# Ending a mixture-of-experts kernel with accumulating DMAs into the output, and splitting the last four scatters over two sums

## The reference, cut to what matters

```
x = x + attention(ctx_512, layernorm(x))
xn = layernorm(x)
routed = zeros(T, 512)
for e in experts:                       # 64
    routed[token_of[e]] += (silu(g) * u) @ down[e] * weight[e]    # g, u = xn[token_of[e]] @ gate_up[e]
shared = silu(xn @ shared_gate.T) * (xn @ shared_up.T) @ shared_down.T
x = x + routed + shared                 # 2048 x 512 float32, 4 MiB
```

## Time and profile before

| | us |
|---|---|
| median of 3 runs | 582.22 (580.47 to 582.86) |
| the profiled execution's own time | 581.39 |
| its span in the trace | 579.8 |
| busy: PE, DVE, ACT, POOL | 536.4, 245.3, 161.8, 224.6 |
| last scatter issued | 547.84 |
| first load of the even sum issued | 552.79 |
| last addition on DVE ends | 573.55 |

### The profile page before, as it was taken

How to read it: one execution, slowest core, us unless ns; L and a number is a source line. 1 busy time by engine, 2 the same in 40 slices (tenths; PEclk the granted TensorE clock), 3 DMA queues, 4 the chain that set the end, 5 groups by cost and what they waited for, 6 DMA issues and landing times.

```text
span 579.8 us, 6266 instructions
## 1 busy us (share of the span) xinstructions
PE 536.4 (93%) x2087; PEld 290.6 (50%) x2087; DVE 245.3 (42%) x641; ACT 161.8 (28%) x342; POOL 224.6 (39%) x221
## 2 busy tenths in 40 slices
PE   4999999678799999999999999999999999999835
PEld 2545545444355555555555555555555555554312
DVE  0786779999612232222222321223222322325535
ACT  3775797673011111211111111111211111120000
POOL 3052155642343354434444444434633363432200
PEclk9999999999999999999999999999999999999969
DMA  8947386789277999989999999999999999868487
GB/s 278 355 167 274 85 290 222 278 300 364 65 271 210 312 280 303 285 261 327 286 278 308 329 299 274 331 277 269 316 300 273 303 308 326 224 121 261 90 298 298
DMA packets 53704, 155.06 MB, mean 267 GB/s; under 512 B 7264, under 2 KB 8800, under 8 KB 52128
## 3 DMA queue, kind: packets, MB, share of 16 engines
q1 hardware_dynamic: 34944, 109.74, 52.3%
q0 software_dynamic: 16320, 40.39, 30.1%
q10 hardware_dynamic: 2400, 4.46, 2.2%
HBM read 116.28 MB, written 38.28 MB: 267 GB/s over the span
## 4 chain that ended last, share of the span: by engine, by line
PE 57%; DMA 18%; DVE 10%; issue 8%; SPq 2%; ACT 2%; POOL 2%; POOLq 0%; DVEq 0%; ACTq 0%
PE bank L870 22%; DMA out<-y,table 12%; PE bank L727 7%; PE bank L738 6%; PE bank L855 4%; PE bank L829 4%; PE bank L640 4%; PE bank L852 3%; PE bank L845 3%; DMA raw_down<-in_sh_down 3%; DMA odd_sum<-y,table 3%; DVE bn L1130 1%; DVE x L1127 1%; PE bank L836 1%; DVE ones_hi L1192 1%
## 5 line engine op out<-in xcount | busy, mean ns | idle before, releaser
L870 PE MATMUL bank<-gu_w,gxT 128*128 128x384 f32 x512 | 178.9, 493 | 2.2 <-ACT gxT L1058 2.2
L870 PEld LDWEIGHTS bank<-gu_w,gxT 128*128 128x128 f32 x512 | 93.2, 190 | 79.8 <-issue 28.9
L563 POOL DMA_INDIRECT out<-y,table x34 | 54.1, 1591 | 199.6 <-DVE y L1360 166.2
L1346 DVE TENSOR_TENSOR hid<-bank,eg 128x192 f32<-128x192 f32 x64 | 22.9, 358 | 178.9 <-ACT eg L1066 178.9
L1066 ACT ACTIVATE eg<-bank 128x192 f32<-128x192 f32 x64 | 21.2, 332 | 275.6 <-PE bank L870 275.6
L727 PE MATMUL bank<-xnT,upT 128*128 128x512 f32 x192 | 86.2, 595 | 1.6 <-ACT sg L973 1.5
L569 POOL DMA_INDIRECT gx<-rows_dram,table x64 | 63.1, 985 | 27.7 <-issue 19.2
L1360 DVE TENSOR_SCALAR y<-bank,gx 128x512 f32<-128x512 f32 x64 | 45.1, 746 | 54.1 <-PE bank L855 54.1
L640 PE MATMUL bank<-w,h1T 128*128 128x512 f32 x128 | 57.7, 593 | 0.0
L738 PE MATMUL bank<-downT,shid 128*128 128x512 f32 x96 | 44.9, 611 | 11.6 <-DVE shid L1232 11.6
L727 PEld LDWEIGHTS bank<-xnT,upT 128*128 128x128 f32 x192 | 34.9, 190 | 39.1 <-issue 36.4
(11 more groups left out here) (179 smaller groups left out, 511.5 us busy)
## 6 DMA issues: line engine op xcount, KB each, us to landing
gu_w<-in_gate_up SPq DMA_DIRECT2D x64, 768.0 KB, 6.8
dn_w<-in_down SPq DMA_DIRECT2D x32, 768.0 KB, 5.4
x<-in_x SPq DMA_DIRECT2D x4, 1024.0 KB, 14.0
feat_dram<-feat SPq DMA_DIRECT2D x16, 256.0 KB, 3.4
out<-shid SPq DMA_DIRECT2D x8, 512.0 KB, 4.1
odd_sum<-shid SPq DMA_DIRECT2D x8, 512.0 KB, 4.9
rows_dram<-rows ACTq DMA_DIRECT2D x4, 1024.0 KB, 10.0
gu_w<-out SPq DMA_DIRECT2D x4, 1024.0 KB, 8.1
```

The costliest lines, as they stand in the source:

```text
L563: pool.indirect_dma_start(sums[lane(e)], bass.IndirectOffsetOnAxis(ap=table[:, e:e + 1], axis=0), y[:, e % YB, :], None, compute_op=ALU.ad ...
L870: last = nc.tensor.matmul(GU[e % 2][:, 0:2 * I], gxT[:, e % 2, c, :], gu_w[:, e % U, c, :], start=(c == 0), stop=(c == KC - 1))
```

## The change: what it does

- `LAST` is 2: experts 60 and 61 still alternate between the lanes, and only 62 and 63 go both to lane 0.
- The even sum is no longer loaded, and x is no longer stored. When all scatters have landed, POOL adds `k.x` to what stands in the output, by accumulating DMAs: one for each of batches 0 to 2 (128 rows of 8 KB), and two for batch 3 (128 rows of 4 KB each). These DMAs wait for `merged` (x has shared part and odd sum) or, for batch 3, for `x3_ready`.
- SP's loads of the odd sum of batches 2 and 3 both follow the second `sent`.
- DVE's order at the end is new: 16 additions of the even sum are gone, and the merge of batch 3's odd sum stands behind that of batch 2.
- The load of `W0` moves from SP's queue to the head of ACT's.

```diff
-LAST = 4
+LAST = 2
...
-                def store_last(h):
...
-                def store_out(b):
-                    sp.wait_ge(total_ready, (b + 1) * TB)
-                    sp.dma_start(a["out"][b * N:(b + 1) * N, :].rearrange("(p t) d -> p t d", t=TB),
-                                 k.x[:, b * TB:(b + 1) * TB, :]).then_inc(out_stored, 16)
...
-                sp.dma_start(w0[:].rearrange("f (h o) -> f h o", h=H),
-                             a["W0"].rearrange("h f o -> f h o")).then_inc(w0_in, 16)
...
-                sp.wait_ge(sent, 1)
+                sp.wait_ge(sent, 2)
                 load_sum(1, 2)
-                sp.wait_ge(sent, 2)
                 sp.wait_ge(y_ready, E - YB + TB)
                 sp.wait_ge(added[0], 16 * sum(lane(d) == 0 for d in range(E - YB + TB)))
                 load_sum(1, B - 1)
-                sp.wait_ge(added[0], 16 * in_lane[0])
-                sp.wait_ge(y_ready, E)
-                for b in range(B):
-                    load_sum(0, b)
-                for b in range(B - 1):
-                    store_out(b)
-                for h in range(2):
-                    store_last(h)
...
+                def add_to_out(first, tiles):
+
+                    here = slice(first % TB, first % TB + tiles)
+                    b = first // TB
+                    pool.dma_start(a["out"][b * N:(b + 1) * N, :].rearrange("(p t) d -> p t d", t=TB)[:, here, :],
+                                   k.x[:, first:first + tiles, :], accum_op=ALU.add).then_inc(k.out_stored, 16)
...
                 for j in range(2):
                     pool.wait_ge(added[j], 16 * in_lane[j])
+                for b in range(B - 1):
+                    pool.wait_ge(merged, (b + 1) * TB)
+                    add_to_out(b * TB, TB)
+                for h in range(2):
+                    pool.wait_ge(x3_ready, NT - TB // 2 + h * TB // 2)
+                    add_to_out(NT - TB + h * TB // 2, TB // 2)
...
+                act.dma_start(w0[:].rearrange("f (h o) -> f h o", h=H),
+                              a["W0"].rearrange("h f o -> f h o")).then_inc(w0_in, 16)
...
                 def shared_down(t):
                     dve.wait_ge(sdn_done, t + 1)
-                    if t >= NT - TB // 2:
-                        dve.wait_ge(total_ready, t + 1)
-                    elif t >= NT - TB:
-                        dve.wait_ge(merged, 2 * TB)
+                    if t >= NT - TB:
+                        dve.wait_ge(merged, t + 1)
...
                 last = B - 1
+                shared_up(last, 0)
                 merge(1, 0)
-                shared_up(last, 0)
-                merge(1, last)
                 merge(1, 1)
                 shared_up(last, 1)
                 merge(1, 2)
-                merge(0, 0)
+                merge(1, last)
                 shared_up(last, 2)
-                merge(0, 1)
-                shared_down(last * TB)
-                merge(0, 2)
-                shared_down(last * TB + 1)
-                merge(0, last)
-                shared_down(last * TB + 2)
-                shared_down(last * TB + 3)
+                for t in range(last * TB, NT):
+                    shared_down(t)
```

More of the change, by code:

```diff
@@ L1384, in _, with merge @@
                 judge()
-                def merge(j, b):
+                def merge(j, b, tiles=range(TB)):
                     dve.wait_ge(sum_in[j][b], 16)
[L1388 to L1391, removed]
+                    for n in [b * TB + t for t in tiles]:
+                        if b < B - 1:
                             dve.wait_ge(x3_ready, n + 1)
                         nc.vector.tensor_tensor(k.x[:, n, :], k.x[:, n, :], part_of(j, b)[:, n - b * TB, :],
-                                                ALU.add).then_inc((total_ready, merged)[j], 1)
+                                                ALU.add).then_inc(merged, 1)
                 last = B - 1
+                shared_up(last, 0)
                 merge(1, 0)
-                shared_up(last, 0)
-                merge(1, last)
                 merge(1, 1)
```

## The result

The changed kernel took 578.3 us (median of 19 runs, 575.76 to 581.67) against 582.03 (19 runs): ratio 0.9948, 95% interval 0.993 to 0.9966. It is faster by 0.5%, where 8.1 us or 1.4% were forecast.

A forecast was written before the change was run, and what follows sets the result against it. The last scatters' chain, then the additions to the output, were taken to set the end: 547.8 + 23.3 + 0.6 = 571.7. 579.8 - 571.7 = 8.1 us off the median 582.22 gave 574.1 us, range 571.3 to 582.5.

The forecast's parts named there:

- the other path: Kernel's end, x of batch 3: POOL issues the last half at 564.0, end through the branch at 570.6.
- the sum: Kernel's end: additions' data end at 571.1, landed 0.6 later at 571.7, against 579.8 before: 8.1 us off.
- rival 4: The two lanes give nothing: scatters 62 and 63 take 9.0 us each beside the loads; 577.7 us, chance 0.07.
- The scatter chain: Scatters of experts 60 to 63: the last lands at 545.0, where it was 552.8; first addition issued at 545.7.
- The rate of the additions: Additions to the output at the end: 4.19 MB at 180 GB/s take 23.3 us, from 547.8 on.
- Rivals 1 and 2: Additions at the lone scatter's mean, 32.0 us (582.8, chance 0.09); or not following closely, 36.8 us (587.6, chance 0.10).
- x of batch 3: Last `shared_up` at 552.7, then 24 matmuls on PE: x complete at 563.9, 1.1 us to spare on this path.
- Rival 3: x of batch 3 ends the kernel: odd sum's loads 2 us late, clock fallen; 576.6 us, chance 0.14.
- W0: First 29 us: an earlier W0 gives the first products slack, not the kernel; taken as 0, either way up to 0.5.

The follow-up runs named there:

- The plain store by POOL: The kernel before, with only the last half of batch 3 stored by POOL instead of SP, without accumulation: 586.91 us, ratio 1.0103.
- the version that waits first: The changed kernel, with POOL waiting for all five additions to have landed before the end of the block: 581.24 us, ratio 1.0008.
- the version with loads and stores in the best order: The kernel before with two lanes, W0 on ACT, new order, last `shared_up` ahead of the even sum's merges, no additions in DRAM: 573.11 us, ratio 0.9842.
- the version of plain stores: The changed kernel with POOL's five DMAs as plain stores, the even sum left out of the result: 574.97 us, ratio 0.9892.

## Why the prediction was wrong

**The step that failed** is the end of the other path: "POOL issues the last half at 564.0; such an issue takes 0.75 us where SP's took 0.33, so the end through the branch is 564.0 + 6.2 + 0.4 = 570.6", and with it the sum that ends 0.6 us behind the last data, with the landing. The 6.2 us from SP's last issue to the end held no wait for the transfer. I carried them over to a DMA of POOL. But POOL's part of the block's end is a drain, which ends 1.5 us past the landing (569.6, drain over at 571.1), and flag, branch and what lies between add 5.1 us. Forecast from landing to end: 0. Measured: 6.6 us. The landing itself came 2.1 us sooner than forecast (569.6 for 571.7), and these two make the 4.5 us by which the span missed (576.2 for 571.7). The kernel before showed a warning that I did not read, on its line 322:

```profile
L322 POOLq DRAIN  x1: 3825/3825/3825, 553.0 to 553.0; - x1
```

There it lay 20 us ahead of the others and cost nothing. The plain store by POOL shows that it takes no accumulation (1% slower), the version that waits first that the drain has 4.2 us of its own, and the version without flag, branch and general code that the 5 us behind it are these. No run has the additions without POOL's drain at the end, so that the whole 6.6 us would have come back without it is not shown. The measured 578.3 lies near what rivals 3 and 4 gave (576.6 and 577.7), but by neither's mechanism.

**The scatter chain: right.** Expert 60 took 4.9 us (chosen 4.73), 61 5.88 (5.1), 62 about 4.7 (7.2 chosen; the loads came too late to disturb it), 63 8.7 (7.2). The first addition came 2.1 us sooner than forecast, 0.9 of these from the start of the kernel. Taking the lanes back from the changed kernel costs 0.7% (1.0022 against 0.9948), more than the whole gain; rival 4 is out. That they are worth so much only together with DVE's new order (0.9977 alone) the prediction did not say.

**The rate of the additions: the total right, in part by luck.** I took 180 GB/s and 23.3 us from first to last data; measured were 23.2 us and 180 GB/s. But "the rate of a queue that has work" was 215 GB/s, with 8 KB rows and nothing beside them. The time that this saved went elsewhere: at first the loads of the odd sum still shared the engines (0.32 MB after 545.7), and the last 6 us of additions ran at 129 GB/s. In the version with four scatters in one lane, where four additions stood ready together, 557 to 577.3 us moved 4.07 MB, 200 GB/s. Rivals 1 and 2 (131 and 114 GB/s) are out. The Trainium skill ("Collectives: The Full Stack", "The bandwidth ceiling: the fold count and why AG ≠ RS ≠ AR") tells of two source reads for the adding step of a ReduceScatter, a collective between cores; applied to these additions, as the prediction did, its half agrees with the trace where the queue was full: plain rows reached 422 GB/s, half of which is 211. "So some 22 us of loads and stores are replaced by 23 us of additions" was, at the full rates, 20 by 19.5: I read no gain from that by itself, and none shows, since the version with loads and stores in the best order is 1.1% faster than the change, and its last data landed sooner behind the last scatter by 2 us.

**x of batch 3: right in its times, not in its margin.** PE waited 1.7 us (3.5 forecast) and kept the full clock, 10.57 us for the 24 matmuls (10.5), the last addition issued at 563.16 (564.0). Rival 3's late loads and fallen clock did not come. But "the additions set the end, with 1.1 us to spare on this path" does not fit: POOL had waited 4.32 us for x before the last issue, and the addition ahead of it landed at 565.9 (558.01 + 7.9), about when the data of the last half could begin (2.1 us behind its issue, as the prediction took it from the scatter: 565.3). So the two paths came together, and x of batch 3 had nothing to spare.

**W0: near.** Taken at 0; the loads were 2.6 us sooner, the last experts 0.86, and the two measurements of it (0.9994, and 0.995 against 0.9948) do not tell it from 0. My reason was wrong, though: the raw weights did land sooner, so the bytes ahead of them were not all that held them.

## What to carry to other kernels

Ask of the last DMA not only when its data land but what the program's end waits for: a DMA of POOL near the end of the block held all engines at its drain here until 1.5 us past the landing, and what followed the block (5.1 us) came on top, where a DMA of SP let its landing run beside it (SP's drain: 0.13 us). An addition in DRAM cost the DMA engines here about what a load and a store cost (215 against 422 GB/s at their best); it took 16 additions off DVE, and whether it pays where DVE is the bound no run shows. And shortening a chain of DMAs needs a look at the in-order engine behind it: putting what PE waits for ahead of the merges of the even sum took 0.8% off here (0.9922 to 0.9842).

## What the runs showed that I had not expected

- POOL's drain takes 3.8 us in the kernel before, where it begins 0.2 us after its last DMA has landed, and ends 1.4 to 1.9 us past the landing where it begins right behind the issue (571.1 for 569.6, 577.4 for 575.9, 570.7 for 569.3, 579.3 for 577.7, and 568.9 for 567.0 in the version of plain stores). What it does in that time no row shows.
- Stores of SP and additions of POOL together slow each other unevenly: three additions took up to 20.9 us to land, with the load and the stores of batch 3 beside them, against 14.1 in the changed kernel.
- The twelve down products at 150 us took 5.4 us in some executions and 6.8 to 7.1 in others, with a granted clock over 5 us of 1.00 before and of 0.66 in the changed kernel and in that with W0 back on SP, in kernels whose work there is the same: slow in six of the fourteen traces. What decides it is not shown. Such a difference (1.5 us) can be in any comparison of single traces here; the medians of many executions suffer less from it.
